# The sums of the last four node tiles in two hops, gathered row by row instead of multiplied

## The reference, cut to what matters

```python
def hop(h):                                   # third layer: called twice
    return segment_sum(norm[:, None] * h[src], dst, num_segments=N)
agg = segment_sum(feat_n[src], dst, num_segments=N)      # fourth layer
rst = (agg @ weight) * (in_deg ** -0.5)[:, None] + bias
```

## Time and profile before

| | us |
|---|---|
| median of 3 runs | 4840.89 (4840.52 to 4844.62) |
| the profiled execution: its own time | 4833.84 |
| its span, first to last instruction | 4832.1 |
| dense phase, first matmul (L1442) to the end of the span | 3999.7 to 4832.1 |
| hop 0 / hop 1 / hop 2, last matmul | 4216.3 / 4510.6 / 4820.9 |

### The profile page before, as it was taken

The page is one execution under the profiler, slowest core; times in us unless marked ns, Lnnn a source line. Parts: engine busy times, 40 slices in busy tenths (PEclk is TensorE's granted clock), DMA queues, the critical chain, the costliest instruction groups (busy, mean ns, idle before and its releaser), DMA issues.

```text
span 4832.1 us, 65140 instructions
## 1 busy us (share of the span) xinstructions
PE 3550.9 (73%) x23472; PEld 2787.2 (58%) x23472; DVE 2500.4 (52%) x6348; ACT 948.6 (20%) x2714; POOL 2375.8 (49%) x2521
## 2 busy tenths in 40 slices
PE   3676677666736666667667577777777779999999
PEld 2444455444524444445445355455555569999999
DVE  3555556555626666666666355555555553222211
ACT  0100000000102222232223222223222220011111
POOL 4566666666466666666664656665555540000000
PEclk9777778787868888888888777878898889999999
DMA  5333232323233333333332222233333337777775
GB/s 139 87 73 71 61 72 64 73 60 72 51 71 92 102 93 102 92 104 91 102 92 79 61 73 68 77 85 95 98 106 100 103 92 245 281 267 266 260 265 214
DMA packets 192382, 555.53 MB, mean 115 GB/s; under 512 B 77640, under 2 KB 83243, under 8 KB 172522
## 3 DMA queue, kind: packets, MB, share of 16 engines
q1 hardware_dynamic: 67136, 335.46, 21.7%
q0 software_dynamic: 80432, 124.45, 12.5%
q10 hardware_dynamic: 44538, 92.03, 5.1%
HBM read 455.05 MB, written 96.37 MB: 114 GB/s over the span
## 4 chain that ended last, share of the span: by engine, by line
PE 46%; another core or an unknown queue 23%; DVE 14%; issue 9%; ACT 6%; DMA 2%; ACTq 1%; DVEq 0%; SPq 0%
PE banks L1442 16%; PE banks L1188 8%; PE banks L1216 6%; DVE scan L2249 4%; PE banks L1148 4%; DVE hot_lo L1912 3%; PE banks L1350 2%; PE banks L1145 2%; ACT adj L1674 2%; PE banks L1162 2%; PE banks L1358 2%; DVE hot_hi L1914 2%; DVE back L2254 2%; ACT adj L1673 1%
## 5 line engine op out<-in xcount | busy, mean ns | idle before, releaser
L906 POOL DMA_INDIRECT gath<-table,ids x2496 | 2364.3, 947 | 1554.9 <-issue 671.9
L1216 PE MATMUL banks<-hot_key,hot_src 128*128 128x392 bf16 x1600 | 472.4, 383 | 721.7 <-ACT adj L1674 501.9
L1188 PE MATMUL banks<-back 128*96 128x104 f32 (+11 forms) x6000 | 800.9, 286 | 101.2 <-issue 48.3
L1188 PEld LDWEIGHTS banks<-back 128*96 128x96 f32 x6000 | 743.0, 198 | 171.5 <-issue 150.1
L2278 DVE TENSOR_SCALAR hot_key<-banks,key_t 128x392 bf16<-128x392 int16 x1600 | 658.8, 412 | 327.1 <-remote 275.4
L1442 PE MATMUL banks<-r_parts,adj_in 128*128 128x288 bf16 x6543 | 810.0, 287 | 5.6 <-DMA adj_in<-adjacency 4.4
L1442 PEld LDWEIGHTS banks<-r_parts,adj_in 128*128 128x128 bf16 x6543 | 802.4, 143 | 8.4 <-issue 4.2
L1216 PEld LDWEIGHTS banks<-hot_key,hot_src 128*128 128x128 bf16 x1600 | 147.8, 109 | 1028.6 <-issue 973.7
L2249 DVE TENSOR_TENSOR_SCAN scan<-keep_of,scan,banks 96x512 f32<-96x512 bf16 x414 | 526.4, 1271 | 229.0 <-remote 129.3
L1148 PE MATMUL banks<-ea_of,w_edge_of 128*96 128x512 f32 x832 | 522.3, 710 | 14.4 <-issue 13.2
L1673 ACT ACTIVATE adj<-banks 128x160 bf16<-128x160 f32 x800 | 240.5, 301 | 1178.8 <-remote 640.4
(11 more groups left out here) (175 smaller groups left out, 2497.8 us busy)
## 6 DMA issues: line engine op xcount, KB each, us to landing
adj_in<-adjacency SPq DMA_DIRECT2D x114, 1568.0 KB, 6.6
adjacency<-adj ACTq DMA_DIRECT2D x100, 464.0 KB
gath<-table,ids POOLq DMA_INDIRECT x2496
ea_of<-in_ea_t SPq DMA_DIRECT2D x78, 512.0 KB
keep_of<-keep_max_d SPq DMA_DIRECT2D x52, 768.0 KB
adjacency<-adj ACTq DMA_DIRECT2D x100, 320.0 KB
adj_in<-adjacency SPq DMA_DIRECT2D x33, 928.0 KB, 4.8
ahead_of<-adjacency SPq DMA_DIRECT2D x33, 640.0 KB
```

The lines of the kernel that those rows point to most:

```text
L906: pool.indirect_dma_start(gath[:, b, t, :], None, tables[p][:, :], bass.IndirectOffsetOnAxis(ap=ids[:, 1, n:n + 1], axis=0),).then_inc(s_g ...
L1188: m = pe.matmul(band_ps[g % 2][:, at:at + n], rows_in[:, q % 2, t * D:(t + 1) * D], hot_dst[:, q % 2, t, first:first + n], start=False, st ...
L1216: m = pe.matmul(window_ps, hot_src[:, 2 * (k % 2) + j, a, :], hot_key[:, 2 * (k % 2) + j, a, :], start=a == 0, stop=a == KEY_TILES - 1)
```

## The change

The four last real tiles (45 to 48, `SLOT_AT` = 45) no longer get their sums from TensorE in hops 1 and 2. GpSimd gathers instead, for each of these 512 nodes, up to 42 neighbour rows (`SLOTS`) from a table in DRAM, by 42 x 4 = 168 indirect DMAs of 128 rows of 384 bytes in each hop; a slot beyond a node's last edge reads row 6399, which is zero. A batch is 3 slots of the 4 tiles, 12 DMAs; there are 14 batches, and two buffers for them. VectorE adds each batch up (`add_slots`, three additions over 384 columns), one batch beside each unit of TensorE. Of the 168 x 128 slots, (42 - 17.3) / 42 = 59% read row 6399: counted from the inputs 4 to 8% in batches 0 to 3, then 21, 44, 73, 91 and 97% in batches 4 to 8, and 99 to 100% in batches 9 to 13.

The indices come from the list of keys that the sparse phase left in DRAM: VectorE works out the places (`slot_places`), GpSimd fetches 168 times 128 pairs of 8 bytes during hop 0, and VectorE turns them into row numbers after hop 0 (`slot_sources`, six operations on 168 columns). The two tables are new stores: ScalarE writes every unit of rows after hop 0 and after hop 1 (`store_r` and in `normalise_x`; 17 stores each). The units of hops 1 and 2 are now: fourteen of three tiles by TensorE (0 to 41), tiles 45 to 47 and tile 48 by slots, and last tiles 42 to 44 by TensorE. At the start VectorE also makes sure that no node has over 42 edges (two operations on 32 partitions x 860, one small one); otherwise the other path is taken.

```diff
+SLOT_TILES, SLOTS = 4, 42
+SLOT_AT = HI - SLOT_TILES
+EACH = 3
+BATCHES = SLOTS // EACH
+SLOT_UNITS = {BATCHES: (SLOT_AT, 3), BATCHES + 1: (SLOT_AT + 3, 1), BATCHES + 2: (SLOT_AT - 3, 3)}
+FIRST_SUM = (0, HI, HI + SLOT_AT)
+FIRST_UNIT = (0, UNITS, 2 * UNITS - 2)
+SLOT_PARTITIONS = 96
...
+            slot_ix = sb("slot_ix", [P, SLOT_TILES, SLOTS], I32, dense)
+            slot_got = sb("slot_got", [P, SLOT_TILES, SLOTS, 2], at=dense)
+            slot_src = sb("slot_src", [P, 2, SLOT_TILES, SLOTS], at=dense)
+            slot_rows = sb("slot_rows", [P, 2, EACH, SLOT_TILES, D], at=dense)
+            slot_sum = sb("slot_sum", [P, SLOT_TILES, D], at=dense)
...
+        def over_units(eng, peeled, *stages, by_slots=True):
+
+            whole = BATCHES if by_slots else TRIOS
 
             def step(i, b, known):
                 for stage, lag in stages:
                     t = 2 * i + b - lag if known else None
                     if not known or 0 <= t < UNITS:
-                        stage(i + (b - lag) // 2, (b - lag) % 2, 1 if t == UNITS - 1 else 3)
+                        w = 3 if not known or t < whole else SLOT_UNITS[t][1] if by_slots else 1
+                        stage(i + (b - lag) // 2, (b - lag) % 2, w)
             for s in range(peeled):
...
+        def first_of(i, b):
+
+            return SLOT_UNITS[2 * i + b][0] if type(i) is int and 2 * i + b >= BATCHES else 3 * (2 * i + b)
...
-                    with sp.Fori(AHEAD_TRIOS if n == 0 else 1, TRIOS) as t:
+                    with sp.Fori(AHEAD_TRIOS if n == 0 else 1, TRIOS if n == 0 else BATCHES + 1) as t:
                         for j in range(3):
                             load_adjacency(n, t, j)
-                    load_adjacency(n, TRIOS, 0)
+                    if n == 0:
+                        load_adjacency(n, TRIOS, 0)
                 sp.wait_ge(d_out[0], 16 * (TRIOS // 2 + 1))
...
+
+                pool.wait_ge(s_key_ix, 2)
+                key_pairs = bass.AP(key_runs.tensor, key_runs.offset, [[2, KEY_READS * KEY_COPY * RUN // 2], [1, 2]])
+                for s in range(SLOTS):
+                    for j in range(SLOT_TILES):
+                        pool.indirect_dma_start(
+                            slot_got[:, j, s, :], None, key_pairs,
+                            bass.IndirectOffsetOnAxis(ap=slot_ix[:, j, s:s + 1], axis=0),
+                        ).then_inc(s_key_got, 16)
+
+                pool.wait_ge(s_key_ix, 3)
+                for n in (1, 2):
+                    for b in (0, 1):
+                        pool.wait_ge(s_table[n][b], 16 * ((BANDS + 1) // 2 + UNITS // 2 + 1 - b))
+                    for c in range(BATCHES):
+                        k = BATCHES * (n - 1) + c
+                        if k >= 2:
+                            pool.wait_ge(s_taken, BANDS + k - 1)
+                        for s in range(EACH):
+                            for j in range(SLOT_TILES):
+                                pool.indirect_dma_start(
+                                    slot_rows[:, c % 2, s, j, :], None, tables[n][:, :],
+                                    bass.IndirectOffsetOnAxis(ap=slot_ix[:, j, EACH * c + s:EACH * c + s + 1], axis=0),
+                                ).then_inc(s_gath[c % 2], 16)
...
+                            if n == 2:
+                                sources = sources[:SLOT_AT - 3] + sources[SLOT_AT:] + sources[SLOT_AT - 3:SLOT_AT]
+                                ready.update({h: g + 1 for g, (h, _) in SLOT_UNITS.items()})
...
-                                if j == min(1, w - 1):
+                                if j == 1:
                                     multiply(i + (b - 1) // 2, (b - 1) % 2, 3)
+                            if n == 2 and known and t == BATCHES and j == 1:
+                                turn_nodes(i, b, 3)
 
...
-                        over_units(pe, 2, (unit, 0))
+                        for s in range(2):
+                            unit(0, s, 3)
+                        with pe.Fori(1, BATCHES // 2) as i:
+                            unit(i, 0, 3)
+                            unit(i, 1, 3)
+                        unit(BATCHES // 2, 0, 3)
...
-                turn_nodes(TRIOS // 2, 0, 1)
-                multiply(TRIOS // 2, 0, 1)
+                multiply(BATCHES // 2, 0, 3)
+                for t in (BATCHES + 1, BATCHES + 2):
+                    turn_nodes(t // 2, t % 2, SLOT_UNITS[t][1])
+                    multiply(t // 2, t % 2, SLOT_UNITS[t][1])
...
+                def store_r(i, b, w):
+                    act.wait_ge(d_r[1], 2 * i + b + 1)
+                    act.dma_start(tiles_in_order(tables_v[1], i, b, w), tiles_in_order(r_sb, i, b, w)).then_inc(s_table[1][b], 16)
...
+                    act.wait_ge(d_norm[1], 2 * i + b + 1)
+                    act.dma_start(tiles_of(tables_v[2], i, b, w), tiles_of(r_sb, i, b, w)).then_inc(s_table[2][b], 16)
...
+                over_units(act, 4, (store_r, 0), by_slots=False)
+                for b in (0, 1):
+                    act.wait_ge(s_table[1][b], 16 * ((BANDS + 1) // 2 + UNITS // 2 + 1 - b))
...
+            crowded = y[SLOT_PARTITIONS:P, :, :, :].rearrange("p b t f -> p (b t f)")[:, 0:NEAR - SLOTS]
+            ve.tensor_tensor(crowded, near(1)[SLOT_PARTITIONS:P, 0:NEAR - SLOTS], near(1)[SLOT_PARTITIONS:P, SLOTS:NEAR], ALU.is_equal)
+            ve.tensor_reduce(sq[SLOT_PARTITIONS:P, 0, 0:1], crowded, AX.X, ALU.max)
+            ve.tensor_tensor(falls[SLOT_PARTITIONS:P, :], falls[SLOT_PARTITIONS:P, :], sq[SLOT_PARTITIONS:P, 0, 0:1], ALU.max)
...
+                    if n > 0 and by_slots(i, b):
+                        at = first_of(i, b) - SLOT_AT
+                        ve.tensor_copy(to[:, b, 0:w, :], slot_sum[:, at:at + w, :])
+                        ve.drain()
+                        return
+                    last = n > 0 and type(i) is int and 2 * i + b == UNITS - 1
+                    ve.wait_ge(d_mm, FIRST_SUM[n] + (SLOT_AT if last else 3 * (2 * i + b) + w))
...
+                def slot_places():
+
+                    for half in (0, 1):
+                        ve.wait_ge(s_adj[half], 32 * 2 * BUILT)
+                    ve.wait_ge(s_window_mm, WINDOWS * BUILT * 2)
+                    ve.scalar_tensor_tensor(slot_ix[:, :, :], start_at[:, SLOT_AT:HI].unsqueeze(2).to_broadcast([P, SLOT_TILES, SLOTS]),
+                                            float(RUN // 2), iota_i[:, 0:SLOTS].unsqueeze(1).to_broadcast([P, SLOT_TILES, SLOTS]),
+                                            ALU.add, ALU.add).then_inc(s_key_ix, 1)
...
+                def slot_sources():
+
+                    ve.wait_ge(s_key_got, 16 * (SETS + SLOT_TILES * SLOTS))
+                    key, low = slot_got[:, :, :, 0], slot_got[:, :, :, 1]
+                    inside, source = slot_src[:, 0, :, :], slot_src[:, 1, :, :]
+                    ve.tensor_tensor(key, key, slot_key[:, :].unsqueeze(2).to_broadcast([P, SLOT_TILES, SLOTS]), ALU.subtract)
+                    ve.drain()
...
+                def add_slots(n):
+                    def stage(i, b, w):
+                        if type(i) is int and 2 * i + b >= BATCHES:
+                            return
+                        rows_in = [slot_rows[:, b, s, :, :] for s in range(EACH)]
+                        ve.wait_ge(s_gath[b], 16 * (QT * PAIRS * SPARSE + EACH * SLOT_TILES * (BATCHES // 2 * (n - 1) + i + 1)))
+                        ve.tensor_tensor(rows_in[0], rows_in[0], rows_in[1], ALU.add)
+                        if type(i) is int and 2 * i + b == 0:
+                            ve.drain()
+                            ve.tensor_tensor(slot_sum[:, :, :], rows_in[0], rows_in[2], ALU.add).then_inc(s_taken, 1)
+                            return
+                        ve.tensor_tensor(slot_sum[:, :, :], slot_sum[:, :, :], rows_in[2], ALU.add)
+                        ve.drain()
+                        ve.tensor_tensor(slot_sum[:, :, :], slot_sum[:, :, :], rows_in[0], ALU.add).then_inc(s_taken, 1)
+                    return stage
...
-                over_units(ve, 4, (hop_one, 0))
-                over_units(ve, 4, (hop_two, 0), (factors(1), 0), (parts_two, 1))
-                over_units(ve, 4, (scale_in, 0), (finish, 1), (factors(2), 1))
+                slot_places()
+                over_units(ve, 4, (hop_one, 0), by_slots=False)
+                slot_sources()
+                over_units(ve, 4, (add_slots(1), 1), (hop_two, 0), (factors(1), 0), (parts_two, 1))
+                over_units(ve, 4, (add_slots(2), 1), (scale_in, 0), (finish, 1), (factors(2), 1))
```

More of the change, by code:

```diff
@@ new lines, in slot_sources @@
+                def slot_sources():
[4 more added lines that the diff above has]
+                    ve.drain()
+                    ve.tensor_scalar(inside, key, -0.5, None, ALU.is_gt)
+                    ve.scalar_tensor_tensor(source, key, float(P), low, ALU.mult, ALU.add)
+                    ve.drain()
```

(7 more changed lines are left out.)

45 lines of the change are left out of this document (26 added, 19 removed).

## The result

The change made the kernel **slower**: 5306.4 us (5288.5 to 5307.8, four runs) against 4840.7, a ratio of 1.0962, 95% interval 1.0944 to 1.098. The prediction said 4810 and at most 4881.

A forecast was written before the change was run, and what follows sets the result against it. TensorE was taken to bound the dense phase; -48.6 + 2.35 + 2.5 + 4.9 + 1.5 + 6 = -31.3 us gave 4802.5 on the profiled execution's 4833.84, or 4810 on the median 4840.9, range 4796 to 4881.

The forecast's parts named there:

- From hop 0 to hop 1: hidden, 0: Turn to hop 1: the 168 pair reads and `slot_sources` finish before TensorE needs them, costing 0.
- The DMA term of hop 0 (+1.5): Hop 0: pair reads raise the DMA engines' share from 0.79 to 0.98, delaying loads of counts: +1.5 us.
- Do the gathers keep pace?: Hops 1 and 2: batches take 15 us, pad batches 18.0, against 18.4 per unit; cost 0 up to 1.7 us per pad gather.
- The padded gather: Late batches of hops 1 and 2: gathers of one row take 1.5 us, 0.5 of the DMA engines; +6 us.
- the second rival: DMA engines overflow: pairs cost hop 0 up to 20 us, pad gathers 17; 4815 to 4832 us, typically 4824; chance 0.18.
- The third rival: Hops 1 and 2: pad gathers get slower beside loads; 4881 us at 2.2 us a gather; chance 0.34.
- TensorE's work, -48.6: Hops 1 and 2: 392 matmuls go, saving 48.0 us, and 0.6 of transposes and products leaves the stream.
- The start, +2.35: Start of kernel: VectorE's check for crowded nodes, which TensorE waits for, adds 2.35 us that nothing covers.
- Between the hops, +2.5: Hop 1 to hop 2: TensorE loses 3.9 us waiting for the last unit's parts instead of 1.4: +2.5 us.
- The tail, +4.9: End of kernel: three units follow the last matmul, taking 16.0 to 16.1 us instead of 11.2: +4.9 us.
- VectorE, 0: Hops 1 and 2: three additions per unit, 1.9 us in 18.4 with drains, hidden at 30% busy: 0.
- The signs of being wrong: TensorE waiting for `adj_in` or `r_parts` over 10 us together, or the sparse phase moving by more than 2.35 us.

The follow-up runs named there:

- e8: Kernel before plus extra gathers of plain 384-byte rows in the dense phase, four per tile up to a run of 64: 5062.0 us beside 4833.3.
- e7: Changed kernel with 24 reads of 7 pairs in hop 0, padded slots reading separate zero rows, four gathers per TensorE tile: 4819.8 us beside 4833.3.
- e6: Changed kernel with 24 reads of 7 pairs in hop 0 and padded slots reading separate zero rows, batches of 12 unpaced: 5043.7 us beside 4833.3.
- e13: As e7, but padded slots read row 6399 again: 4882.3 us beside 4789.2.
- e12: e7 again, on another chip, with rounds: 4773.4 us beside 4790.8, ratio 0.9971.
- e5: The changed kernel again, unedited, on another chip: 5273.7 us beside 4833.3 for the kernel before.
- e16: Kernel before plus the extra gathers of e8 in the same pattern, but 8 bytes a descriptor: 5005.9 us beside 4789.2.
- e9: e6 with a drain and a memset on GpSimd behind every four gathers of hops 1 and 2: 5034.7 us beside 4790.8, ratio 1.0503.
- e11: Kernel before with three drains and memsets on GpSimd behind every four gathers of the sparse phase: 6239.6 us beside 4790.8.

## Why the prediction was wrong, point by point

- **"From hop 0 to hop 1: hidden, 0", wrong by 216 us.** The step that failed is the one that asked only whether the 168 reads are in time. They were (the last one began at 4221.5, with 4215 forecast for its end, inside the 15 us of lead; the first began at 4009.9 and not at 4005), `slot_sources` waited for nothing, and yet TensorE stood still beside them. I took an engine that does nothing else for one that disturbs no one. What the runs showed in its place: beside 168 gathers in a row TensorE does next to nothing from 10 us after their start until 23 us after their end, and 215.9 us are lost. The DMA term of hop 0 (+1.5) was not tested, since no run has 168 reads beside a TensorE at full rate; its price was too high, 0.24 us of the engines for a read that took 0.06.
- **"Do the gathers keep pace?" Yes**, and more easily than I said: L972 took 944 ns at the median and VectorE's L2607 waited 1.1 us in all. But a batch of 12 was one uninterrupted run of 15 us, 24 times, and the first two batches of a hop one of 24. By the table of e8 that is 24 x 8.2 + 2 x 25.1 = 247 us; e7 has one run of 12 and eight of 8 left, 31 us, and e6 against e7 gives 218 in the two hops. The sum had no term for this.
- **The padded gather: the mechanism was right, the term (+6) mis-sized.** I gave it 0.5 us of the engines, from the earlier trace rows, where nothing ran beside it. Beside loads it took 1.19 in the change and 0.93 in e13. With it my own sum gives 0.74 x 18.4 + 12 x 1.19 = 27.9 us of engines against 18.4 for a unit, 67 in seven, 133 in both hops; e13 lost 109. This is the mechanism of the second rival at about twice its price for a gather (whose own sum, 4810 - 7.5 + 37 = 4839, was also 7 us above the 4832 given). The third rival got the other thing wrong: the gathers slowed the loads, not GpSimd. The Trainium skill ("HBM Reference", Latency) has an access take ten times as long at high load; measured was 1.9 to 2.4 times the 0.5 us of an idle time, in share of the engines.
- **TensorE's work, -48.6: right.** There are 6151 matmuls, and a unit of hop 2 in e12 takes 18.98 us as before. Where neither loss is (e12), hops 1 and 2 take 581.6 us instead of 604.6. The forecast was 604.6 - 48.6 + 2.5 = 558.5; most of the 23 missing are the run of 12 at the start of hop 1 (6.7 us), 0.4 to 0.6 for most further units of it, the turn to hop 2, and the last unit of hop 2, which by VectorE's reduction takes 22.3 us.
- **The start, +2.35: right in size.** The first gather begins at 43.0 instead of 40.7. The other 2.7 us of the sparse phase are within what it varies by: on one chip it ended at 3995.3 in e5, 4003.2 in e6 and 3997.2 in e7.
- **Between the hops, +2.5: right.** TensorE waits 4.1 us for `r_parts` instead of 1.3. **The tail, +4.9: right**, as the earlier trace rows: the last matmul with counts starts at 5269.9, and the span ends 16.8 us later; before 11.5.

```profile
5273.28 1.06 DVE L2572 TENSOR_REDUCE agg<-banks 128x288 f32<-128x864 f32 x1
...
5280.81 0.46 DVE L2650 TENSOR_TENSOR v<-banks,x_sb 128x288 f32<-128x288 f32 x1 [3.16 <-PE banks L1480]
...
5284.35 0.38 ACTq L1924 DMA_DIRECT2D out_x<-y  x1
```

- **VectorE, 0: right.** L2607 takes 558 ns, as the earlier trace rows.
- **The signs of being wrong** that the prediction named both came: TensorE waited 38.5 us for `adj_in` and 4.1 for `r_parts`, over 10 together, and the sparse phase moved by 5.0. Neither names the larger loss.
- **The range was too narrow by a whole cause.** All my rivals priced the new work on its own engine and on the DMA engines. The profile of before had what may be a hint, and I passed over it because the change doesn't touch it: in the sparse phase TensorE's weight loads were idle for 973.7 us before "issue". There GpSimd works in runs of eight (219 of them) and of four.

## What to carry to other kernels

Work given to an idle GpSimd isn't free for the others: on chips that behave like this one, break gathers up into groups of four, each waiting for something that another engine does anyway, never with a drain, and see that they don't merge at the start of a stage. Let padded gathers read as many different rows as there are partitions. When a large part of an engine's idle time is put down to "issue", find out what its neighbours do at that time before more of the same is added.

## What the runs showed that I had not expected

- A run of gathers on GpSimd holds up TensorE, on the chip of the result and on three of the four chips of the experiments: nothing is lost for about 10 us, then TensorE does 36 matmuls in 100 us, and it stays so for 23 us after 168 gathers, with GpSimd and the DMA engines idle. What is shared is not settled: the records have no wait for it. The DMA engines' load is not it (0.10), nor the size of a descriptor (e8 and e16). The queue of instructions has ten packets of 16 KB between 4020 and 4240 us before (row below); the change has none there, and the next only at 4246, when TensorE is back at full rate. So these don't tell whether missing instructions are the cause or TensorE simply asked for none. That something is piled up fits the time behind the run, and e9, where a drain took 3.8 us on average after a gather's record had ended. The Trainium skill ("Perfetto Trace Analysis", DMA Instruction — SWDGE (GPSIMD)) has the record end with the last descriptor written; the drains show that GpSimd wasn't free then.

```profile
q8 instruction: 10, 0.16, 0.3%
```

- It depends on the chip. The kernel before took 4841 us where the result was measured and 4789 to 4833 on three chips of the experiments, but 4070 on the fourth, the difference being in the sparse phase alone; on that one a run of 64 gathers cost nothing. Whether the sparse phase is slow on the others by its own runs of eight (219 of them, at 2.8 us some 610 of the 760 us) fits, as does that the fourth chip ran on beside runs of 800, but it was not shown, since e11's drains cost more than the runs could. Why the chips differ is open.
- 128 descriptors that read one row take six times as much of the DMA engines as 128 that read different ones (0.93 against 0.15 us), and more beside loads than alone.
